# Two large graph aggregations: VectorE works on a unit of eight slots in two halves of four

## What is computed

```python
# layer 0: 8 heads of 32 channels; layer 1 is alike, with 4 heads of 64 channels
Wh = (x @ W.T).reshape(N, H, C)
e = leaky_relu(e_left[src] + e_right[dst], 0.2)
e_exp = exp(e - segment_max(e, dst)[dst])
alpha = e_exp / (segment_sum(e_exp, dst)[dst] + 1e-16)
out = segment_sum(Wh[src] * alpha[:, :, None], dst)      # [N, H * C]
```

## Time and profile before

| | us |
|---|---|
| median of 3 runs | 10117.94 |
| runs | 10090.75 to 10120.89 |
| profiled execution, first to last instruction (its own time is given by this span alone) | 10110.4 |
| VectorE busy | 5594.3 (55%) |
| GpSimd busy | 5337.1 (53%) |
| TensorE busy | 2288.8 (23%) |
| ScalarE busy | 1093.7 (11%) |

### The profile page before, as it was taken

The page is one execution under the profiler, slowest core; times in us unless marked ns, Lnnn a source line. Parts: engine busy times, 40 slices in busy tenths (PEclk is TensorE's granted clock), DMA queues, the critical chain, the costliest instruction groups (busy, mean ns, idle before and its releaser), DMA issues. The chain is left out here.

```text
span 10110.4 us, 54577 instructions
## 1 busy us (share of the span) xinstructions
PE 2288.8 (23%) x9111; PEld 1752.0 (17%) x9112; DVE 5594.3 (55%) x8828; ACT 1093.7 (11%) x2533; POOL 5337.1 (53%) x5411
## 2 busy tenths in 40 slices
PE   2112000000000002146555512000000000129995
PEld 1111000000000001135444411000000000116663
DVE  8764588788777677523333275455656556421111
ACT  1101000000000001112222201000000000002221
POOL 0025656666676654455555345776666777542221
PEclk7555555555555555578777755555555555559997
DMA  4051333433333353411111162433333333620004
GB/s 142 22 159 50 97 82 87 122 99 98 101 101 98 102 113 74 122 23 33 29 28 28 30 172 89 109 100 92 101 98 101 106 99 99 129 97 30 30 30 117
DMA packets 458121, 869.43 MB, mean 86 GB/s; under 512 B 175134, under 2 KB 294860, under 8 KB 448192
## 3 DMA queue, kind: packets, MB, share of 16 engines
q0 software_dynamic: 239536, 575.99, 23.0%
q1 hardware_dynamic: 167648, 182.04, 6.2%
q10 hardware_dynamic: 50788, 110.02, 3.3%
HBM read 693.35 MB, written 180.71 MB: 86 GB/s over the span
## 5 line engine op out<-in xcount | busy, mean ns | idle before, releaser
L914 POOL DMA_INDIRECT agg_ring<-table,agg_idx x4320 | 4275.8, 990 | 2329.8 <-issue 1323.4
L1042 DVE TENSOR_TENSOR agg_part<-agg_ring,agg_prob 128x2048 f32 x420 | 964.4, 2296 | 631.8 <-issue 556.2
L1080 DVE TENSOR_TENSOR agg_wide<-agg_wide,agg_part 128x2048 f32<-128x2048 f32 x420 | 960.4, 2287 | 14.4
L1786 PE MATMUL dense_tp<-all_ident,dense_xn 128*128 128x128 f32 x100 | 23.9, 425 | 2570.3 <-issue 2543.7
L1408 PE MATMUL agg_hp<-agg_xt,agg_w 128*128 128x256 f32 x1600 | 446.4, 439 | 579.4 <-ACT agg_ht L1378 340.3
L2208 DVE TENSOR_TENSOR experts_h<-experts_sg,experts_hp 128x682 f32<-128x682 f32 x106 | 91.8, 866 | 779.7 <-ACT experts_sg L2191 779.7
L2158 PE MATMUL experts_hp<-mixture_w,experts_xt 128*128 x1696 | 518.2, 458 | 0.6 <-ACT experts_xt L2187 0.6
L1408 PEld LDWEIGHTS agg_hp<-agg_xt,agg_w 128*128 128x128 f32 x1600 | 352.4, 224 | 663.8 <-ACT agg_ht L1378 360.4
L1786 PEld LDWEIGHTS dense_tp<-all_ident,dense_xn 128*128 128x128 f32 x100 | 20.3, 228 | 2571.9 <-issue 2544.5
L2129 POOL DMA_INDIRECT yc<-experts_ysb,experts_list x105 | 103.7, 987 | 685.2 <-DVE experts_ysb L2217 685.2
L1422 PE MATMUL agg_yp<-agg_w,agg_ht 128*128 128x256 f32 x1600 | 405.3, 411 | 231.0 <-remote 174.5
(11 more groups left out here) (421 smaller groups left out, 6520.8 us busy)
## 6 DMA issues: line engine op xcount, KB each, us to landing
agg_ring<-table,agg_idx POOLq DMA_INDIRECT x4320
y<-agg_ysb ACTq DMA_DIRECT2D x25, 1024.0 KB
rank_y<-y SPq DMA_DIRECT2D x10, 2560.0 KB
rank_x<-x SPq DMA_DIRECT2D x30, 640.0 KB
copies<-first_sort_words SPq DMA_DIRECT2D x16, 1024.0 KB
copies<-last_sort_words ACTq DMA_DIRECT2D x16, 1024.0 KB
x<-rank_x SPq DMA_DIRECT2D x20, 640.0 KB
agg<-agg_res ACTq DMA_DIRECT2D x98, 128.0 KB
```

Source lines behind the costliest of these rows:

```text
L914: pool.indirect_dma_start(out=self.ring[:, to:to + self.RW], out_offset=None, in_=self.table, in_offset=bass.IndirectOffsetOnAxis(ap=index ...
L1042: return dve.tensor_tensor(to[:, :].rearrange("p (j h c) -> p j h c", j=UNIT, h=H), ring[:, ds(st.at(at_u), UNIT * RW)].rearrange("p (j w) ...
L1080: dve.tensor_tensor(wide[:, :], wide[:, :], part[:, :], ALU.add).then_inc(widened, 1)
```

## The change

The loop of `tile` handles slots 0 to 3 and 4 to 7 of a unit with instructions of their own. The order is multiply low, multiply high, add low, add high. The low half has two new semaphores, `low_taken` and `low_widened`; GpSimd still waits for `taken`, which the high half's multiply raises. After the loop VectorE waits for both halves. The tail's `weigh` stays whole.

The sizes of a tile become six 16-bit values: the first slot is split into its quotient and remainder by 16, and put together again in registers.

```diff
+LOAD = 6
...
-        sizes = s.sb("sizes", [1, 5 * (NT + 1)], I32)
+        sizes = s.sb("sizes", [1, LOAD * (NT + 1)], mybir.dt.uint16)
+        bits, split = s.sb("bits", [1, 2 * (NT + 1)], I32), s.sem("split")
...
+        low_taken, low_widened = s.sem("low_taken"), s.sem("low_widened")
...
-            ng, nk, c0, k0, missing = nc.values_load_multi_w_load_instructions(sizes[0:1, ds(t * 5, 5)], engines=[eng.engine], min_val=0, max_val=cfg.max_slots,
-                                                                      skip_runtime_bounds_check_because=why)[1]
-            return nc.s_assert_within(ng, 1, CH, skip_runtime_bounds_check_because=why), nk, c0, k0, missing
+            ng, nk, c_high, c_low, k0, missing = nc.values_load_multi_w_load_instructions(
+                sizes[0:1, ds(t * LOAD, LOAD)], engines=[eng.engine], min_val=0, max_val=cfg.max_slots, skip_runtime_bounds_check_because=why)[1]
+            return nc.s_assert_within(ng, 1, CH, skip_runtime_bounds_check_because=why), nk, c_high * SLOTS + c_low, k0, missing
...
-                of_tile = sizes[:, :].rearrange("p (t w) -> p t w", w=5)
+                of_tile = sizes[:, :].rearrange("p (t w) -> p t w", w=LOAD)
+                bits2 = bits[:, :].rearrange("p (t w) -> p t w", w=2)
+                dve.tensor_scalar(bits2[:, :, 0], st.inf[:, I_C0:I_C0 + NT + 1], 4, None, ALU.logical_shift_right).then_inc(split, 1)
+                dve.tensor_scalar(bits2[:, :, 1], st.inf[:, I_C0:I_C0 + NT + 1], SLOTS - 1, None, ALU.bitwise_and).then_inc(split, 1)
...
-                for w, first in ((1, I_NK), (2, I_C0), (3, I_K0)):
-                    dve.tensor_copy(of_tile[:, :, w], st.inf[:, first:first + NT + 1]).then_inc(sized, 1)
+                dve.tensor_copy(of_tile[:, :, 1], st.inf[:, I_NK:I_NK + NT + 1]).then_inc(sized, 1)
+                dve.tensor_copy(of_tile[:, :, 4], st.inf[:, I_K0:I_K0 + NT + 1]).then_inc(sized, 1)
...
+                dve.wait_ge(split, 2)
+                dve.tensor_copy(of_tile[:, :, 2:4], bits2[:, :, :]).then_inc(sized, 1)
...
+                dve.sem_inc(low_taken, cfg.RU - 1)
+                dve.sem_inc(low_widened, cfg.RU)
...
+                def weigh_half(at_u, u, half):
+                    j0 = half * (UNIT // 2)
+                    return dve.tensor_tensor(part[:, j0 * CW:(j0 + UNIT // 2) * CW].rearrange("p (j h c) -> p j h c", j=UNIT // 2, h=H),
+                                             ring[:, ds(st.at(at_u) + j0 * RW, UNIT // 2 * RW)].rearrange("p (j w) -> p j w", w=RW)[:, :, 0:CW].rearrange("p j (h c) -> p j h c", h=H),
+                                             prob[:, ds(u * UH + j0 * H, UH // 2)].rearrange("p (j h) -> p j h", h=H).unsqueeze(3).to_broadcast([P, UNIT // 2, H, C]),
+                                             ALU.mult)
...
+                            dve.wait_ge(low_widened, n)
+                            weigh_half(n, u + first, 0).then_inc(low_taken, 1)
                             dve.wait_ge(widened, n)
-                            weigh(n, u + first, part).then_inc(taken, 1)
+                            weigh_half(n, u + first, 1).then_inc(taken, 1)
+                            dve.wait_ge(low_taken, n)
+                            dve.tensor_tensor(wide[:, 0:UC // 2], wide[:, 0:UC // 2], part[:, 0:UC // 2], ALU.add).then_inc(low_widened, 1)
                             dve.wait_ge(taken, n)
-                            dve.tensor_tensor(wide[:, :], wide[:, :], part[:, :], ALU.add).then_inc(widened, 1)
+                            dve.tensor_tensor(wide[:, UC // 2:UC], wide[:, UC // 2:UC], part[:, UC // 2:UC], ALU.add).then_inc(widened, 1)
...
+                        dve.wait_ge(low_widened, n1)
                         dve.wait_ge(widened, n1)
```

More of the change, by code:

```diff
@@ L1027, in _ @@
                 dve.wait_ge(st.info_in, 16)
-                of_tile = sizes[:, :].rearrange("p (t w) -> p t w", w=5)
+                of_tile = sizes[:, :].rearrange("p (t w) -> p t w", w=LOAD)
+                bits2 = bits[:, :].rearrange("p (t w) -> p t w", w=2)
+                dve.tensor_scalar(bits2[:, :, 0], st.inf[:, I_C0:I_C0 + NT + 1], 4, None, ALU.logical_shift_right).then_inc(split, 1)
+                dve.tensor_scalar(bits2[:, :, 1], st.inf[:, I_C0:I_C0 + NT + 1], SLOTS - 1, None, ALU.bitwise_and).then_inc(split, 1)
                 dve.tensor_scalar(of_tile[:, :, 0], st.inf[:, I_NG:I_NG + NT + 1], 1.0, None, ALU.max).then_inc(sized, 1)
-                dve.tensor_scalar(of_tile[:, :, 4], st.inf[:, I_NK:I_NK + NT + 1], -1.0, 4096.0, ALU.mult, ALU.add).then_inc(sized, 1)
-                for w, first in ((1, I_NK), (2, I_C0), (3, I_K0)):
-                    dve.tensor_copy(of_tile[:, :, w], st.inf[:, first:first + NT + 1]).then_inc(sized, 1)
+                dve.tensor_copy(of_tile[:, :, 1], st.inf[:, I_NK:I_NK + NT + 1]).then_inc(sized, 1)
+                dve.tensor_copy(of_tile[:, :, 4], st.inf[:, I_K0:I_K0 + NT + 1]).then_inc(sized, 1)
+                dve.tensor_scalar(of_tile[:, :, 5], st.inf[:, I_NK:I_NK + NT + 1], -1.0, 4096.0, ALU.mult, ALU.add).then_inc(sized, 1)
+                dve.wait_ge(split, 2)
+                dve.tensor_copy(of_tile[:, :, 2:4], bits2[:, :, :]).then_inc(sized, 1)
                 dve.wait_ge(const, 5)
```

## The result

The kernel after takes 10191.82 us (median of 5 runs, 10186.98 to 10203.09) against 10117.94 (10090.75 to 10138.21): a ratio of 1.0072, 95% interval 1.0057 to 1.0088. It is slower by 0.7%, 74 us. The forecast was slower by 171 us. The profiled execution took 10186.98 us, and its instructions span 10185.1.

What follows compares the result with a forecast made beforehand. VectorE's own sequence was taken to bound the first aggregation, its slow sequencer's instruction count the slow stretch of the second; -84 - 20 + 5 + 71 + 199 = +171 us on 10117.94 gave 10,289 us, range 9,990 to 10,560.

Steps and rivals of the forecast that it cites:

- its own case: Whole kernel: slower, from 10,150 to 10,480 us, with two quick tiles to one slow or the reverse; chance 0.45.
- The price of the halves in a slow unit: Looped unit under the slow sequencer: four added instructions at 0.7 to 1.0 us each, nothing hiding them, 3.4 us a unit.
- One slow tile to one quick: Second aggregation: slow tiles of 64.4 us alternate with quick ones of 44.1, 4.85 us more a tile, 199 us over 41.
- The first aggregation: First large aggregation: halves -84 us, loads -20, late slow units +71; forecast change of the stage -28 us.
- The loop's term: First aggregation, quick sequencer: 161 hidden gaps of 0.44 us save 71 us, overlapping halves 13 us, 84 us together.
- 21 slow looped units: First aggregation's two late slow stretches: 10 and 11 looped units lose 3.4 us each, 71 us.
- The loads: Sizes' load on VectorE, first aggregation: six 16-bit values take 0.4 us less a tile, 49 tiles, 20 us gained.
- the rule of the Trainium skill: Halves, first aggregation: without overlap, 4.90 us a unit, saving 12 us, a sum 72 us higher; the prediction rejected it.
- A: Rival, second aggregation: GpSimd's longer idle times don't restore the sequencer, always slow; 10,705 us; chance 0.12.
- B: Rival: added instructions cost nothing more when slow; second aggregation unchanged, first keeps 99 us gain; 10,019 us; chance 0.31.
- C: Rival: 99 us gain meets 71 us and a little more of loss; 10,090 to 10,148 us; chance 0.12.

Runs made afterwards that it cites:

- T: Follow-up chip whose sequencer goes slow: the kernel before took 10105.83 us, the whole change against it 10195.19 us, ratio 1.0079.
- the increments: Kernel before with the new sizes, loop whole, and three semaphore increments that nobody waits for in each looped unit: 10284.93 us, ratio 1.0173 on T.
- R: Follow-up chip whose sequencer goes slow: kernel before 10100.02 us; against it five 16-bit sizes, loop whole, 1.0005; halves in the first aggregation with four for VectorE, 0.9998.
- P: Follow-up chip with a quick sequencer: kernel before 9118.76 us; against it sizes alone 1.0024, with halves in the first aggregation only 0.9967, in the second only 1.0040.
- Q: Follow-up chip with a quick sequencer: the kernel before took 9116.56 us, the whole change against it 9100.98 us, ratio 0.9982.

## Why the prediction was right and wrong

The direction was right on this chip and on T, and so was the mechanism of the second aggregation: the loss comes from more sequencer instructions under a sequencer that goes slow, and GpSimd's longer pauses end the slow stretches more often. The measured 10,192 us lie in the span that the prediction gave its own case. But the sum was off by 97 us, and two errors in it go opposite ways: the second aggregation lost 34 us instead of 199, and the first lost 34 instead of gaining 28. With the first as forecast the kernel would have been some 12 us slower, too little to be told. So the direction came out clearly through a loss that the prediction didn't have.

**The price of the halves in a slow unit** (3.4 us, for "a multiply, an add and two address instructions more"): measured 1.3 us (6.89 to 8.16). This is the step that failed. The prediction divided 6.8 us by seven instructions and put about 1 us on each, the multiply and the add among them. In a slow stretch vector instructions cost nothing of their own: the 6.9 us are five register and branch instructions at 1.4 us, and the 4.6 us of vector work lie beside them. Halves add two vector instructions, which are free there, and one address instruction, not two: 1.4 us. That nothing hides an added instruction was right; what was wrong is which instructions count, how many of them the halves add, and the price of each. A slow tile so grew by 6.7 us with four looped units (47.1 to 53.8) and by 7.4 with five (54.7 to 62.1) instead of by 15.0; one instruction of that growth, some 1.4 us a tile, stands outside the loop.

**One slow tile to one quick** (+4.85 us a tile): measured 96 slow units to 65 quick. The recovery is real: 130 slow units of 161 before, 96 after, 76 with the increments. But a slow tile of 54 to 62 us leaves GpSimd pauses of at most 15 us, not 20, and only 10 of 18 pauses of 8 us or more turned VectorE quick, where the longer ones of the increments (mostly 15 to 17 us) did in 15 of 17. 96 x 8.16 + 65 x 4.54 is 1079 us against 1054 before (161 x 6.55): +25 of the stage's +34. The other 9 us lie outside the loops.

**The first aggregation** (-84 for the halves, +71 for late slow units, -20 for the loads): measured +34. The loop's term was exact on quick chips, 85 us for 84. Two things were missing. About 31 us of it comes back as waits for ScalarE, which the prediction didn't look for because the stage was "VectorE's own sequence". And on a chip with the slow sequencer the halves bring the slow stretches forward. The first slow VectorE instruction of the stage comes at 3063 us before and 2095 after; on T at 2914 with the loop whole and 2197 with halves, on R at 2804 and 2174. There they hit all that VectorE does, not the looped units alone: on T the loops are 53 us shorter than with the loop whole (161 intervals, 5.21 to 4.88 us), and still the stage is 30 us longer. Of the 83 us lost outside the loops, 42 are idle time before steps of the sort (`last_sort_words`), by the instructions by line. Pricing only 21 slow looped units missed these.

**The loads** (0.4 us shorter, 20 us gained): 0.43 us longer, 21 us lost. Among 16-bit loads the number of values sets the time, and fewer bytes gained nothing: five 16-bit values take 1.17 us, longer than the 1.04 of five 32-bit ones in the mean. The Trainium skill (Runtime: NRT & Kernel Launch, "Instruction fetch mechanics") puts a register load at about 200 ns per register even in bulk; the runs agree with 0.22 us for the 16-bit ones. The one-word row of 0.31 us should have been read as one register, not as four bytes.

Not going by the rule of the Trainium skill that the next VectorE operation starts only when the pipe is empty (VectorE: DVE Perf Modes, "The DRAIN you can't avoid") was right here: halves of 1.22 us start 1.13 us apart. The same section adds that an operation that is not held starts earlier, and that is the case that the trace shows.

The rivals: A (no recovery) fell; the quick tiles are there. B (more instructions don't cost more under a slow sequencer) fell as well, with the increments; that the kernel is faster on P's kind of chip has another reason, a sequencer that is never slow, and is far less than its 99 us. C (no change) is not what was measured on this chip, where the ratio is 1.0057 at the least.

## What to carry to other kernels

Before splitting an instruction, read the loop's branch and register instructions in every stage. Where they take 0.7 us, count only register, branch and semaphore instructions, for the whole tile and not for the loop alone, and check the price against the length of several tiles with different counts. Here that gives 1.39 us an instruction, vector instructions free, and the six kinds of slow tile to within about 1%. Cheap instructions that no wait needs cost nothing on one chip and over 60 us in one stage on the next. A gap that is closed on one engine is a gain only up to what the next engine has ready, so list the releasers one step behind it. And load fewer values into registers, not narrower ones.

## What the hardware showed that was not expected

The same program takes 9117 to 9127 us on three chips and 10100 to 10118 on three others (or fewer: the first pair's may be R or T). Nearly all of these 10% lie in the stages that have sequencer instructions of 0.7 us or multiples; behind the second aggregation, where VectorE has none, the slow trace is 18 us longer (1359 against 1341 us). They come in stretches, on VectorE, ScalarE and SyncE (1133, 755 and 47 register and branch instructions over 0.48 us in the second aggregation of the kernel before), and on GpSimd in none of that stage. More sequencer instructions make the stretches costlier and, in the first aggregation, earlier.

In a slow stretch the recorded times of sequencer instructions are not those of their work. The program has both address instructions of a unit before its multiply. In the rows of the slow unit above one of them starts at 7868.8 us and lasts 0.70 us, while the multiply starts at 7868.9. In 107 of 130 slow units of the kernel before two address instructions are recorded as starting behind their multiply, and on a quick chip (Q, the sizes alone) not one in 161 units. So the records lag behind the work there. What makes the sequencer slow stays open. Every execution timed here was also recorded by the profiler, so these runs can't tell whether it belongs to the chip or to the recording on that chip. The Trainium skill (NOTIFIC — the notification-queue block, section 7.1, "Overflow: three behaviours, one of which stalls the engine") says that the block that writes trace records can hold up the engines that produce them. The late records would fit it, but no run here shows whether that is the cause; one without a recording was not made.
